# The ring of the split W3: two slots of 1024 columns in place of four of 512

## The reference

```python
x = x + L0(x, weight, scale_log, codebook, lora_A, lora_B)   # W0 quantised to 8 levels, plus a low-rank part
x = x + L1(x, language, W, Wr, A, B)                         # W1, plus a gated low-rank part (top 2 of 8)
x = x + L2(x, adapter, W, b, lora_As, lora_Bs)               # W2 and bias, plus the row's own adapter
x = x + L3(x, adapter_ids, weight)                           # each of the 8 batch rows has its own 1024 x 1024 W3
```

## Time and profile before

| | |
|---|---|
| median of 3 runs | 689.86 us |
| lowest, highest | 689.34, 691.33 us |
| the profiled execution: its time | 691.96 us |
| the profiled execution: its span | 690.1 us |
| PE busy | 675.9 us, 98% of the span |
| PE weight loads busy | 583.7 us, 85% |
| DVE busy | 349.1 us, 51% |
| ACT busy | 276.9 us, 40% |
| POOL busy | 88.5 us, 13% |
| granted clock of PE, mean | 0.997 of full |

### The profile page before, as it was taken

The page is one execution under the profiler, slowest core; times in us unless marked ns, Lnnn a source line. Parts: engine busy times, 40 slices in busy tenths (PEclk is TensorE's granted clock), DMA queues, the critical chain, the costliest instruction groups (busy, mean ns, idle before and its releaser), DMA issues.

```text
span 690.1 us, 9555 instructions
## 1 busy us (share of the span) xinstructions
PE 675.9 (98%) x3432; PEld 583.7 (85%) x3432; DVE 349.1 (51%) x532; ACT 276.9 (40%) x414; POOL 88.5 (13%) x128
## 2 busy tenths in 40 slices
PE   5899999999999999999999999999999999999998
PEld 5789999999999988788889878889888888888886
DVE  4799889879961364124543222661320653302353
ACT  5656473971813352123651022562121564012353
POOL 2200215005010021001211000311000111000020
PEclk9999999999999999999999999999999999999999
DMA  9932212001000107002874000777000576000263
GB/s 249 323 104 64 59 31 62 1 0 62 1 0 1 62 24 243 2 1 91 280 226 157 0 0 24 246 232 251 0 0 0 181 267 229 16 0 1 91 222 115
DMA packets 39331, 67.61 MB, mean 98 GB/s; under 512 B 3588, under 2 KB 23044, under 8 KB 39300
## 3 DMA queue, kind: packets, MB, share of 16 engines
q1 hardware_dynamic: 34976, 59.33, 27.0%
q10 hardware_dynamic: 4324, 7.87, 3.2%
HBM read 58.80 MB, written 8.39 MB: 97 GB/s over the span
## 4 chain that ended last, share of the span: by engine, by line
PE 92%; DMA 2%; SPq 2%; DVE 1%; issue 1%; ACT 1%; POOL 0%; DVEq 0%; ACTq 0%
PE ps L963 30%; PE ps L964 29%; PE ps L965 29%; DMA e_lo_w<-w_t 2%; PE ps L1082 1%; DMA raw<-w_t 1%; PE ps L976 1%; PE ps L1109 1%; PE ps L978 1%; SPq L399 0%; SPq L343 0%; ACT e_hi L590 0%; POOL e_lo_w L437 0%; SPq L331 0%; PE ps L1091 0%
## 5 line engine op out<-in xcount | busy, mean ns | idle before, releaser
L963 PE MATMUL ps<-e_hi,ring_hi 128*128 128x384 f32 (+3 forms) x384 | 135.0, 352 | 7.8 <-DVE e_lo L702 7.7
L702 DVE TENSOR_TENSOR ring_lo<-raw,ring_hi 128x512 fp32r<-128x512 f32 x128 | 91.0, 725 | 92.1 <-ACT ring_hi L614 92.1
L965 PE MATMUL ps<-e_hi,ring_lo 128*128 128x384 f32 (+3 forms) x384 | 134.6, 351 | 0.0
L614 ACT ACTIVATE ring_hi<-raw 128x512 fp32r<-128x512 f32 x128 | 79.5, 629 | 79.8 <-PE ps L965 61.4
L963 PE MATMUL ps<-x_both,e_hi 128*128 128x512 f32 x256 | 101.8, 398 | 0.0
L964 PE MATMUL ps<-x_both,e_hi 128*128 128x512 f32 x256 | 101.2, 395 | 0.0
L965 PE MATMUL ps<-x_both,e_lo 128*128 128x512 f32 x256 | 100.7, 393 | 0.0
L963 PE MATMUL ps<-ring_hi,e_mid 128*128 128x512 f32 x256 | 99.6, 389 | 0.0
L964 PE MATMUL ps<-ring_lo,e_mid 128*128 128x512 f32 x256 | 99.6, 389 | 0.0
L965 PE MATMUL ps<-ring_hi,e_mid 128*128 128x512 f32 x256 | 99.6, 389 | 0.0
L963 PEld LDWEIGHTS ps<-e_hi,ring_hi 128*128 128x128 f32 x384 | 73.3, 191 | 14.0 <-DVE e_lo L702 8.3
(11 more groups left out here) (143 smaller groups left out, 906.2 us busy)
## 6 DMA issues: line engine op xcount, KB each, us to landing
raw<-w_t SPq DMA_DIRECT2D x64, 512.0 KB, 4.1
xraw<-x_t SPq DMA_DIRECT2D x16, 512.0 KB, 4.6
w_w<-w SPq DMA_DIRECT2D x15, 512.0 KB, 5.1
y<-tmp ACTq DMA_DIRECT2D x30, 256.0 KB, 4.1
e_lo_w<-w_t SPq DMA_DIRECT2D x4, 512.0 KB, 10.9
e_lo_w<-w_t SPq DMA_DIRECT2D x4, 384.0 KB, 5.7
e_mid_w<-bs SPq DMA_DIRECT2D x24, 64.0 KB, 2.4
w_w<-w SPq DMA_DIRECT2D x2, 256.0 KB, 4.0
```

Of the source, the lines that this page charges most:

```text
L614: act.activation(ring_hi[:, (2 * k + h) % 4, :], raw[:, k % RAW, h * 512:(h + 1) * 512], ACT.Copy).then_inc(w3_hi, 1)
L702: return dve.tensor_tensor(out, whole, hi.bitcast(F32), ALU.subtract)
L963: pe.matmul(out, a[0], b_[0], start=start, stop=False, **kw)
L965: return pe.matmul(out, a[1], b_[0], start=False, stop=stop, **kw)
```

## The change

The ring keeps its memory but is used as two slots of 1024 columns. ACT converts a whole tile with one instruction and DVE subtracts with one. All semaphores count tiles, not halves. PE waits once per tile and releases once per tile; it still issues the same 12 matmuls in the same order.

```diff
+        def ring_flat(of, i):
+            return of[:, 2 * (i % 2):2 * (i % 2) + 2, :].rearrange("p a c -> p (a c)")
...
-        X_CREDIT, W3_CREDIT, BS_CREDIT, Y_CREDIT = 2, 2 * RAW, 2, 16
+        X_CREDIT, W3_CREDIT, BS_CREDIT, Y_CREDIT = 2, RAW, 2, 16
...
-                sp.wait_ge(w3_lo, 2 * (16 * g + 8 * j + k + 1))
+                sp.wait_ge(w3_lo, 16 * g + 8 * j + k + 1)
...
             def split_w3(g, j, k):
                 act.wait_ge(w3_diag, 16 * g + 8 * j + k + 1)
-                for h in range(2):
-                    old = 2 * k + h - 4
-                    done = (2 * KT - 2) * (2 * g + j)
-                    if old >= 0:
-                        act.wait_ge(ring_free, done + (2 * KT - 2) + old + 1)
-                    elif old < -2:
-                        act.wait_ge(ring_free, done + (2 * KT - 2) + old + 3)
-                    else:
-                        act.wait_ge(y_mm, 4 * (2 * g + j) + 2 * (old + 3))
-                    act.activation(ring_hi[:, (2 * k + h) % 4, :], raw[:, k % RAW, h * 512:(h + 1) * 512],
-                                   ACT.Copy).then_inc(w3_hi, 1)
+                done = (KT - 1) * (2 * g + j)
+                if k == 1:
+                    act.wait_ge(y_mm, 4 * (2 * g + j) + 4)
+                else:
+                    act.wait_ge(ring_free, done + KT - 1 + max(k - 1, 0))
+                act.activation(ring_flat(ring_hi, k), raw[:, k % RAW, :], ACT.Copy).then_inc(w3_hi, 1)
...
             def split_w3(g, j, k):
-                for h in range(2):
-                    n = 32 * g + 16 * j + 2 * k + h
-                    dve.wait_ge(w3_hi, n + 1)
-                    s4 = (2 * k + h) % 4
-                    minus(ring_lo[:, s4, :], raw[:, k % RAW, h * 512:(h + 1) * 512],
-                          ring_hi[:, s4, :]).then_inc(w3_lo, 1)
+                dve.wait_ge(w3_hi, 16 * g + 8 * j + k + 1)
+                minus(ring_flat(ring_lo, k), raw[:, k % RAW, :], ring_flat(ring_hi, k)).then_inc(w3_lo, 1)
...
-                        ins.then_inc(ring_free, 2 * KT - 2)
+                        ins.then_inc(ring_free, KT - 1)
...
             def y_product(g, j):
+                    pe.wait_ge(w3_lo, W3_CREDIT + 16 * g + 8 * j + k + 1)
                     for h in range(2):
-                        pe.wait_ge(w3_lo, W3_CREDIT + 32 * g + 16 * j + 2 * k + h + 1)
...
-                        if k < KT - 1:
-                            ins.then_inc(ring_free, 1)
+                    if k < KT - 1:
+                        ins.then_inc(ring_free, 1)
```

## The result

The changed kernel takes **692.54 us** (median of 19 runs, 690.76 to 696.49), the kernel before on the same chip 689.58 us (19 runs, 689.10 to 692.20). The ratio is 1.0035, with a 95% interval of 1.0022 to 1.0047: 1.5 to 3.2 us slower. The forecast was 692.3 us.

What follows compares the result with a forecast made beforehand. PE was taken as the bound, busy 675.9 of 690.1 us. Late tiles 1.1, POOL's adds 1.3 and the first group's start 0.1 sum to 2.5 us over the median of 689.86: 692.3 us, range 689.9 to 696.5.

Steps and rivals of the forecast that it cites:

- Where it would be lost, and what stays hidden: PE waits at even tiles of the products; ACT's evacuations, pieces of x and later loads cost nothing.
- S: Start of the last matmul on a slot; the next tile's first weight load is needed at S + 2.72 us.
- The start of the first group: Tiles (0,0) and (0,1) ahead of the gates: between -0.2 and +0.2 us, taken as +0.1.
- The path: Slot release, whole conversion, whole subtraction, weight load: 0.42 + 1.056 + 0.04 + 1.223 + 0.13 = 2.87 us, 0.15 late.
- 0.11 are given back: At PE's late weight load, 0.11 of the 0.15 us lateness is regained, leaving 0.04 us.
- Every second tile: In the products, tiles 2, 4, ..., 14 of each group start late: 7 times in 4 groups, 28 in all.
- The constant part: 28 late tiles in the products at 0.04 us each: 1.1 us, bounds 0 and 4.2.
- POOL's adds: Adds delaying DVE's subtractions: two hits a group, 8 in all, 0.15 to 0.16 us each: 1.3 us, bounds none and 5.8.
- The sum: Whole kernel: 1.1 + 1.3 + 0.1 = 2.5 us more, median 692.3 us.
- It just fits: Rival at even tiles' first weight loads: path 2.83 us or less, stalls vanish, 689.9 to 690.6 us; chance 0.38.
- Paid in full: Rival in the products: PE gains nothing back after a wait, 7.3 us more, 697; chance 0.13.
- The clock: Rival: short waits of PE in the products lower its clock, 19 us more, 709; chance 0.02.

Runs made afterwards that it cites:

- e1: The changed kernel with its one subtraction per tile on DVE cut in two halves; 690.87 us, ratio to the kernel before 1.0006.
- e5: Against the kernel before, only the release is changed, once per tile; conversions and subtractions stay in halves; 690.35 us, ratio 0.9997.
- e2: The changed kernel with POOL's add of the identity to W3 left out; 691.60 us, ratio to the kernel before 1.0016.
- e3: The changed kernel with one small DVE copy between the wait for the conversion and the subtraction; 696.30 us, ratio to the kernel before 1.0079.
- e6: The changed kernel with two half conversions on ACT, then one whole subtraction on DVE; 693.02 us, ratio to the kernel before 1.0041.
- e0: The changed kernel once more, unaltered; 691.67 us, ratio to the kernel before 1.0022.
- e4: The kernel before once more, unaltered; 690.98 us, ratio 1.0005.
- e8: The kernel before with tiles (0,0) and (0,1) converted after x3 tiles 5 and 6, not ahead of the gates; 690.91 us, ratio 0.9993.

## Why the prediction was right, point by point

- **Where it would be lost, and what stays hidden.** Right: the products, and nowhere else. ACT's evacuations, the pieces of x and the later loads cost nothing (no excess in e1 and e5, which have them too; in the changed kernel's first three groups every conversion from the third tile on starts 0.42 to 0.43 us after S, and in all four its subtraction starts 0.03 after its end, whatever stands between). The start of the first group was put at +0.1: from the first x3 matmul to the first product it takes 66.35 us, against 66.56 and 66.07 in the kernel before, nothing that can be told.
- **The path.** Read tile by tile from the changed kernel: 0.43 + 1.06 + 0.03 + 1.23, then 0.05 to the weight load: 2.80 from S in the first three groups, not 2.87. The term that was too long is the step from DVE to PE: 0.05 us, not the 0.13 read after a wait of another kind. With 2.80 the text's own rule ("2.83 or less: the stalls vanish") would have given none. They didn't vanish: the load is 0.08 late, and each tile of the first three groups still loses 0.02 us on average where no add interferes (e2: about 0.3 us over 14 tiles). That "0.11 are given back" and below it nothing is lost was too sharp.
- **Every second tile.** True where lateness is clear (e3, e6: about 0.10 and 0.02 in turn), not in the changed kernel, where odd tiles lose as well as even ones, most of them 0.01 to 0.03. By the prediction's own signs this part failed: it named waits at odd tiles as a sign of being wrong, and it expected 25 to 30 waits and pairs of 44 to 45 us, where the view lists 7 and three of the four pairs are under 44.
- **The last group** loses twice as much (0.58 against 0.30 in e2). There ACT starts 0.48 to 0.49 us after S (644.26 - 643.77), 0.42 to 0.43 in the others, and in its first product the weight load follows the subtraction by 0.12 us in place of 0.05 (646.69 - 645.35 - 1.23 = 0.11 by the lines above). So the path is 2.92 us in the first product and 2.86 in the second. In e2 the first product's tiles 2 to 7 lose 0.35 of the 0.58, the second's eight 0.21. The longer path was not foreseen, and why these two steps are longer there is not known.
- **The constant part** was put at 1.1 us and measures 1.4 (e2, less the kernel before's 0.08).
- **POOL's adds** were put at 1.3 us (8 hits of 0.16) and measure 0.2: this is the term that was mis-sized, and the step that failed is the count of hits, and after it the price of one. In the products the first profile has two subtractions of 1.33 and 1.40 us and one of 1.27, e0 one of 1.36; the others have 1.22 to 1.24. The tiles behind the three of over 1.3 us lose 0.11, 0.06 and 0.10 us, where 0.02 are lost without a hit: 0.04 to 0.09 a hit, not 0.16. Both ends of one hit, in the timelines of DVE and POOL:

```profile
341.17 1.33 DVE L699 TENSOR_TENSOR ring_lo<-raw,ring_hi 128x1024 fp32r<-128x1024 f32 x1 [1.52 <-ACT ring_hi L612]
...
340.96 0.46 POOL L471 TENSOR_TENSOR raw<-raw,ident 128x128 f32<-128x128 f32 x1 [2.67 <-DMA raw<-w_t]
```

The add began 0.21 us ahead and ended 0.25 into the subtraction, which took 0.10 longer. By the rule of the Trainium skill (SBUF — State Buffer, SBUF: two separate sides) that the second waits for the whole of the first it would be 0.25; as in the earlier trace rows the trace gives about 0.15 less. The prediction's remark that by this rule its sum would end about 1 us higher doesn't follow from its own way of counting: 8 hits of half of 0.43 are 1.7 us, 0.4 above its 1.3.
- **The sum.** Predicted 2.5 us over the kernel before; the profiles show 1.6 in the products, and runs with the same kind of start 1.9. That the median came within 0.3 us of the forecast is luck: it owes about 1 us to the mix of starts, since of the 19 runs 10 had the late one (their median is 693.28, that of the others 691.57), and the kernel before's median of 689.58 has the value of an early one (e0's job: 689.55). The direction and the mechanism were right, the sum was a third too large.
- **The rivals.** "It just fits" described the path's length better than the forecast did, and its time (under 0.7 us) less well. "Paid in full" needed nothing given back; 0.12 were. The clock stays at 1.00 through the products, the waits being 0.2 us at most.

## What to carry to other kernels

Merging two operations of a producer chain saves each one's fixed start but adds to the delay from "slot free" to "slot ready"; with two slots that delay must be shorter than the consumer's time on one slot, here 2.72 us against 2.80. So before merging, sum the chain from release to first use, handoffs included, and compare it with (slots - 1) consumer steps (tried here with two slots): engines that are half idle say nothing about it. When only the delay is too long, half of the remedy is enough, if it is the right half: splitting just the last operation (e1) took all of the loss away, splitting just the first (e6) doubled it, since DVE still waited for both halves.

## What the runs showed that was not expected

- A PE that loses 1.6 us in small steps still reads as 100% busy in its windows; here only distances from the start of one matmul to the start of a later one gave the loss.
- A late weight load costs less than its lateness. One that comes 0.08 us past its due time leaves its matmul on time, and the tile loses 0.00 to 0.05 us, 0.02 on average (e2, first three groups); one 0.14 late loses 0.03 on average (e2, last product); one 0.20 late cost 0.08 above. The third group's tile (0,2) in the changed kernel: due at 534.27 + 2.72 = 536.99, here at 537.07, and the matmul on the dot:

```profile
535.79 1.23 DVE L699 TENSOR_TENSOR ring_lo<-raw,ring_hi 128x1024 fp32r<-128x1024 f32 x1 [2.37 <-ACT ring_hi L612]
...
537.07 0.19 PEld L956 LDWEIGHTS ps<-ring_hi,e_mid 128*128 128x128 f32 x1
537.22 0.39 PE L956 MATMUL ps<-ring_hi,e_mid 128*128 128x512 f32 x1
```

- The end of the program, from the start of the last product matmul to the end of the span, takes 4.00 to 4.06 us in the five profiles of kernels with whole conversions on ACT (changed, e0 to e3) and 3.69 to 3.71 in the six with halves (before, e4 to e8), though no instruction there differs. The last transfer of y makes it: 2.36 to 2.42 us from issue to landing in the five, 2.05 to 2.06 in the six. But e0 to e3 are also the runs of chip 4, and e4 to e8 those of chips 0 and 3 (of the two first profiles no chip is on record). The kernel and the chip are not told apart here.
- The wait of 1.1 to 3.0 us at L976 in phase 1 decides over another 1 to 2 us: where the granted clock fell to 0.50 in the next 3 us, the time was 1.2 to 2.3 us longer (the medians of the kernel before at the two kinds of start: 689.55 and 691.88 in e0's job, 689.82 and 691.05 in e4's). From the end of that wait to the first x3 matmul it takes 220.4 us in the six profiles without the fall, 221.9 in four with it and 223.1 in the fifth (e3), where the lower level lasted longer: the fall itself costs 1.5 us, or 2.7. The rest is when the wait ends, from 25.8 to 27.2 us. What makes the clock fall in one execution and not in the next was not tried.
